# Curvature flow: adding K beside H a period later, one clip for both, another order on ScalarE

## What is computed

```python
def step(u, _):
    ux, uy, uxx, uxy, uyy = _derivs(u)            # Sobel stencils, each clipped to [-10, 10]
    g2 = ux * ux + uy * uy
    denK = jnp.maximum(1.0 + g2, EPS)
    K = jnp.clip((uxx * uyy - uxy * uxy) / (denK * denK + EPS), -5.0, 5.0)
    denH = jnp.sqrt(1.0 + g2 + EPS)
    H = ((1.0 + uy * uy) * uxx - 2.0 * ux * uy * uxy + (1.0 + ux * ux) * uyy) / (2.0 * denH ** 3 + EPS)
    H = jnp.clip(H, -5.0, 5.0)
    diff = jnp.clip(alpha * K + beta * H, -1.0, 1.0)
    u = u + DT * diff
    u = jnp.pad(u[:, :, 1:-1, 1:-1], ((0, 0), (0, 0), (1, 1), (1, 1)), mode='edge')
    return (u, None)
u, _ = jax.lax.scan(step, x, None, length=10)
x1 = 0.7 * u + 0.3 * x
out = conv(relu(conv(x1, w1, b1)), w2, b2) + x1
```

## Time and profile before

| | us |
|---|---|
| median of 3 runs | 38702.86 (38694.59 to 38705.76) |
| profiled execution, its own time | 38698.44 |
| its span | 38696.7 |
| PE busy | 34434.2 (89%) |
| DVE busy | 34434.0 (89%) |
| ACT busy | 33167.9 (86%) |
| POOL busy | 20465.8 (53%) |

### The profile page before, as it was taken

The page is one execution under the profiler, slowest core; times in us unless marked ns, Lnnn a source line. Parts: engine busy times, 40 slices in busy tenths (PEclk is TensorE's granted clock), DMA queues, the critical chain, the costliest instruction groups (busy, mean ns, idle before and its releaser), DMA issues. The chain is left out here.

```text
span 38696.7 us, 453600 instructions
## 1 busy us (share of the span) xinstructions
PE 34434.2 (89%) x126400; PEld 23294.9 (60%) x126400; DVE 34434.0 (89%) x33108; ACT 33167.9 (86%) x33722; POOL 20465.8 (53%) x7685
## 2 busy tenths in 40 slices
PE   5888888888888888888888888888888888889999
PEld 3666666666666666666666666666666666666666
DVE  8999999999999999999999999999999999993111
ACT  5999999999999999999999999999999999994333
POOL 3555555555555556555555555555555555550000
PEclk9999999999999999999999999999999999999999
DMA  5333333333333333333333333333333333333333
GB/s 189 83 83 82 82 75 78 83 83 82 82 83 83 82 79 74 81 83 83 83 82 83 83 83 76 77 81 83 83 83 82 83 83 80 73 82 83 87 87 85
DMA packets 2687511, 3261.71 MB, mean 84 GB/s; under 512 B 2266180, under 2 KB 2266308, under 8 KB 2364740
## 3 DMA queue, kind: packets, MB, share of 16 engines
q1 hardware_dynamic: 2686276, 3247.70, 33.5%
HBM read 582.33 MB, written 268.44 MB: 22 GB/s over the span
## 5 line engine op out<-in xcount | busy, mean ns | idle before, releaser
L646 PE MATMUL tame_slot<-tame_split,tame_M 128*128 128x512 f32 x51200 | 15156.1, 418 | 4131.5 <-DVE tame_ux L517 3386.6
L646 PEld LDWEIGHTS tame_slot<-tame_split,tame_M 128*128 128x128 f32 x51200 | 9160.8, 190 | 10140.8 <-issue 2690.5
L646 PE MATMUL tame_slot<-tame_halo,tame_M 128*128 128x512 f32 x51200 | 14319.2, 402 | 0.0
L356 POOL TENSOR_TENSOR tame_split<-tame_U,tame_split 128x1024 fp32r<-128x1024 f32 x2560 | 6232.0, 2434 | 12755.0 <-ACT tame_split L391 12755.0
L646 PEld LDWEIGHTS tame_slot<-tame_halo,tame_M 128*128 128x128 f32 x51200 | 9757.9, 191 | 2513.8
L368 POOL TENSOR_TENSOR tame_ux<-tame_ux,tame_cross 128x1024 f32<-128x1024 f32 x2560 | 8071.5, 3153 | 433.4 <-POOL tame_ux L362 433.4
L362 POOL TENSOR_TENSOR tame_ux<-tame_ux,tame_uy 128x1024 f32<-128x1024 f32 x2560 | 6161.8, 2407 | 972.6 <-DVE tame_uy L517 972.6
L431 ACT ACTIVATE tame_slope<-tame_slope 128x2048 f32<-128x2048 f32 x2560 | 4895.4, 1912 | 0.0
L656 PE MATMUL tame_slot<-tame_uxy,tame_unit 128*128 128x512 f32 x10240 | 4810.6, 592 | 5.4 <-DVE tame_slot L540 5.4
L426 ACT ACTIVATE tame_slope<-tame_slope 128x1024 f32<-128x1024 f32 x2560 | 2716.8, 1061 | 2141.4 <-issue 2139.4
L559 DVE TENSOR_TENSOR tame_uyy<-tame_slot,tame_slope 128x1024 f32<-128x1024 f32 x2560 | 3132.2, 1223 | 945.6 <-PE tame_slot L656 938.1
(11 more groups left out here) (74 smaller groups left out, 38207.5 us busy)
## 6 DMA issues: line engine op xcount, KB each, us to landing
tame_halo<-tame_split SPq DMA_DIRECT2D x2560, 520.0 KB
tame_halo<-tame_split SPq DMA_DIRECT2D x2560, 260.0 KB
tame_halo<-tame_split SPq DMA_DIRECT2D x5120, 65.0 KB
tame_U<-in_x SPq DMA_DIRECT2D x256, 512.0 KB, 3.9
tame_stage<-in_x SPq DMA_DIRECT2D x128, 1024.0 KB, 4.9
mixed<-tame_stage SPq DMA_DIRECT2D x128, 1024.0 KB, 6.4
out<-res SPq DMA_DIRECT2D x672, 192.0 KB
xin<-mixed SPq DMA_DIRECT2D x344, 256.0 KB, 4.6
```

Of the source, the lines that this page charges most:

```text
L356: nc.gpsimd.tensor_tensor(split_rows(c, 1), half_rows(c), split_rows(c, 0).bitcast(F32), ALU.subtract).then_inc(lo_ready, 2)
L646: last = nc.tensor.matmul(ps[name][:, b * BANK:(b + 1) * BANK], M[0:lanes, matrix, :], rows(c, part)[:, b * y:(b + 1) * y, :], start=(n < ...
```

## The change

- K and H are no longer written over `uyy` and `ux2`, but over the two halves of `slope`, where their inverses lie. One `tensor_scalar` over both halves (`clip_both`) clips them, in place of two.
- add_k moves from the end of the period of chunk k-1 to directly ahead of add_h, one period later. add_h waits for it.
- `uyy` has one buffer instead of two; copy_uyy waits for determinant of the chunk before.
- Waits follow the new owners: square_ux for curvature_h, square_slope for add_k, sum_squares for add_h, each two chunks back.
- ScalarE's order is power, log_power, copy_ux, square_ux, inverse_k, inverse_h, scale, high part, square_uy, copy_uyy, square_slope, square_uxy, logs.

```diff
-        ux2, uy2, cross, uyy = pair("ux2"), pair("uy2"), pair("cross"), pair("uyy")
+        ux2, uy2, cross = pair("ux2"), pair("uy2"), pair("cross")
+        uyy = sb("uyy", [P, HALF])
...
             def square_ux(t, c, fresh):
                 if not fresh:
-                    act.wait_ge(updated, done(t, c - 2))
+                    act.wait_ge(h_ready, done(t, c - 2))
...
-            def copy_uyy(t, c, fresh):
+            def copy_uyy(t, c, first):
                 act.wait_ge(ready["uyy"], done(t, c))
-                if not fresh:
-                    act.wait_ge(k_added, done(t, c - 2))
-                nc.scalar.activation(uyy[c % 2][:, :], ps["uyy"][:, :], ACT.Copy).then_inc(uyy_copied, 2)
+                if not first:
+                    act.wait_ge(prod_k, done(t, c - 1))
+                nc.scalar.activation(uyy[:, :], ps["uyy"][:, :], ACT.Copy).then_inc(uyy_copied, 2)
...
             def square_slope(t, c, fresh):
                 act.wait_ge(slope_ready, done(t, c))
                 if not fresh:
-                    act.wait_ge(k_ready, done(t, c - 2))
+                    act.wait_ge(k_added, done(t, c - 2))
...
                 if exists(kind, k):
                     copy_ux(t, k, fresh)
+                    square_ux(t, k, fresh)
+                if exists(kind, k - 1):
+                    inverse_k(t, k - 1)
+                    inverse_h(t, k - 1, kind == "first" and k == 1)
                 if exists(kind, k - 3) and ends(kind, k - 3):
                     scale(r, k - 3)
-                if exists(kind, k - 1):
-                    inverse_k(t, k - 1)
-                if exists(kind, k):
-                    square_ux(t, k, fresh)
-                    square_uy(t, k, fresh)
-                if exists(kind, k - 1):
-                    inverse_h(t, k - 1, kind == "first" and k == 1)
-                if exists(kind, k):
-                    square_slope(t, k, fresh)
-                    copy_uyy(t, k, fresh)
                 if exists(kind, k - 4) and goes_on(kind, k - 4):
                     next_high(t, k - 4, kind, r)
                 if exists(kind, k):
+                    square_uy(t, k, fresh)
+                    copy_uyy(t, k, first)
+                    square_slope(t, k, fresh)
                     square_uxy(t, k, first)
                     logs(t, k)
...
                 if not fresh:
-                    dve.wait_ge(inv_h_ready, done(t, c - 2))
+                    dve.wait_ge(updated, done(t, c - 2))
                 stt(slope[c % 2][:, 0, :], ux2[c % 2][:, :], 1.0, uy2[c % 2][:, :], ALU.add,
                     ALU.add).then_inc(slope_ready, 2)
...
+                K = slope[c % 2][:, 1, :]
+                nc.vector.tensor_tensor(K, ps["uxx"][:, :], K, ALU.mult).then_inc(k_ready, 2)
...
+                nc.vector.tensor_tensor(slope[c % 2][:, 0, :], ux2[c % 2][:, :], inverse[:, :], ALU.mult).then_inc(
+                    h_ready, 2)
+
+            def clip_both(t, c):
+                both = slope[c % 2][:, :, :]
+                dve.wait_ge(k_ready, done(t, c))
                 dve.wait_ge(h_ready, done(t, c))
-                nc.vector.tensor_scalar(Hh, Hh, CURVATURE_CLIP, -CURVATURE_CLIP, ALU.min, ALU.max).then_inc(h_clipped, 2)
+                nc.vector.tensor_scalar(both, both, CURVATURE_CLIP, -CURVATURE_CLIP, ALU.min, ALU.max).then_inc(
+                    both_clipped, 2)
 
             def add_k(t, c):
-                K = uyy[c % 2][:, :]
-                dve.wait_ge(k_clipped, done(t, c))
+                K = slope[c % 2][:, 1, :]
+                dve.wait_ge(both_clipped, done(t, c))
...
             def add_h(t, c):
-                K, Hh = uyy[c % 2][:, :], ux2[c % 2][:, :]
-                dve.wait_ge(h_clipped, done(t, c))
+                K, Hh = slope[c % 2][:, 1, :], slope[c % 2][:, 0, :]
                 dve.wait_ge(k_added, done(t, c))
...
                 if exists(kind, k - 2):
+                    add_k(t, k - 2)
                     add_h(t, k - 2)
...
                     curvature_h(t, k - 1)
-                    clip_k(t, k - 1)
-                    clip_h(t, k - 1)
-                    add_k(t, k - 1)
+                    clip_both(t, k - 1)
```

More of the change, by code:

```diff
@@ L196, in curvature_flow @@
         k_ready = sem("k_ready")
-        k_clipped = sem("k_clipped")
+        both_clipped = sem("both_clipped")
         h_ready = sem("h_ready")
-        h_clipped = sem("h_clipped")
         k_added = sem("k_added")
@@ L539, in determinant @@
             def determinant(t, c):
-                nc.vector.tensor_tensor(ps["uxx"][:, :], uyy[c % 2][:, :], ps["uxx"][:, :], ALU.mult).then_inc(prod_k, 2)
+                nc.vector.tensor_tensor(ps["uxx"][:, :], uyy[:, :], ps["uxx"][:, :], ALU.mult).then_inc(prod_k, 2)
             def term_uyy(t, c):
@@ L558, in curvature_k @@
                 dve.wait_ge(inv_k_ready, done(t, c))
-                nc.vector.tensor_tensor(uyy[c % 2][:, :], ps["uxx"][:, :], slope[c % 2][:, 1, :],
-                                        ALU.mult).then_inc(k_ready, 2)
-            def clip_k(t, c):
-                K = uyy[c % 2][:, :]
-                dve.wait_ge(k_ready, done(t, c))
-                nc.vector.tensor_scalar(K, K, CURVATURE_CLIP, -CURVATURE_CLIP, ALU.min, ALU.max).then_inc(k_clipped, 2)
+                K = slope[c % 2][:, 1, :]
+                nc.vector.tensor_tensor(K, ps["uxx"][:, :], K, ALU.mult).then_inc(k_ready, 2)
             def curvature_h(t, c):
@@ L569, in curvature_h @@
                 dve.wait_ge(inv_h_ready, done(t, c))
-                nc.vector.tensor_tensor(ux2[c % 2][:, :], ux2[c % 2][:, :], inverse[:, :], ALU.mult).then_inc(h_ready, 2)
-            def clip_h(t, c):
-                Hh = ux2[c % 2][:, :]
+                nc.vector.tensor_tensor(slope[c % 2][:, 0, :], ux2[c % 2][:, :], inverse[:, :], ALU.mult).then_inc(
[3 more added lines that the diff above has]
+                dve.wait_ge(k_ready, done(t, c))
                 dve.wait_ge(h_ready, done(t, c))
-                nc.vector.tensor_scalar(Hh, Hh, CURVATURE_CLIP, -CURVATURE_CLIP, ALU.min, ALU.max).then_inc(h_clipped, 2)
+                nc.vector.tensor_scalar(both, both, CURVATURE_CLIP, -CURVATURE_CLIP, ALU.min, ALU.max).then_inc(
+                    both_clipped, 2)
             def add_k(t, c):
-                K = uyy[c % 2][:, :]
-                dve.wait_ge(k_clipped, done(t, c))
+                K = slope[c % 2][:, 1, :]
+                dve.wait_ge(both_clipped, done(t, c))
                 if tame:
```

## The result

The changed kernel takes 45,097.02 us (median, 45,093.32 to 45,103.08), the kernel before 38,698.72 beside it: ratio 1.1654, 95% interval [1.1633, 1.1674]. The forecast was 44,950, the range 43,100 to 46,200. The profiled execution has a span of 45,101.3 us, 6,405 more than that of before.

The account below looks back on a forecast made before the run. VectorE was taken to set the 13.32 us period. Ordinary periods (15.26 + 0.50) added 5,622 us and blended ones 627: 38,698 + 6,249 = 44,947, rounded 44,950, range 43,100 to 46,200.

Parts of the forecast that it names:

- Part 3: add_h on VectorE: L368, issued earlier, takes over and holds it until about 8.08, 2.08 us of waiting.
- Part 1: Merged clip on VectorE: 1.13 us for two starts' 1.20, saving 0.07; its wait for curvature_h adds 0.11.
- Part 2: add_k on VectorE, moved ahead of add_h: it now gives the 0.16 us to L362, ending at 5.97.
- part 4: VectorE after add_h: curvature_k's wait disappears (-0.50 us), sum_squares waits for square_uy (+0.21); ordinary period 15.26 against 13.32.
- Part 5: ScalarE's new order: high part and inverse_h come before they are wanted; cost nothing, covered by about 3 us idle.
- part 7: TensorE pauses about 2.1 us before uxy; half the ordinary periods get a 3.4 us half-speed stretch: +0.5 us per period.
- Part 6: Blended periods: the low part on GpSimd holds the blend 2.4 us more, giving 17.45 us against 15.00.
- Rival A: Handover from add_h to L368 as forecast, but TensorE's clock stays up: 43,800 us, chance 0.22.
- Rival B: Ports stay with VectorE between add_k and add_h, so L368 does not overtake add_h: 38,280 us, chance 0.11.
- C: Same time within 0.2%: add_h not overtaken, but late square_uy or late clip eats the 0.14 gain: 38,700 us, chance 0.04.

Follow-up runs that it names:

- the merge alone: The changed kernel with add_k back at the end of its own chunk's period and ScalarE's old order: 39,753.74 us, ratio 1.0274 to the kernel before.
- the fourth experiment: The changed kernel with the first four matmuls of the uyy product made twice, inside TensorE's pause: 43,977.43 us, ratio 1.1366 to the kernel before.

## Why the prediction was right

By its own steps:

- **Part 3, the handover**, was right in mechanism and size. add_h was to take 3.3 to 3.4 us and took 3.21, 2.0 us of waiting. That L368 takes over before add_h can be issued is shown from three sides: the waiting disappears when L368 is made to wait; it shrinks by 0.94 us when add_h is issued 0.94 later; and it stays, whatever ScalarE's order. From the merge alone to the same kernel with add_k ahead of add_h, the time rises by 5,009 us.
- **Part 1, the clip**: the duration was right (1.23 us against 1.2), the wait mis-sized. I took 0.03 us behind the forerunner's end, from two tiny instructions of the set-up; at full size it is 0.11 to 0.14. That is the 0.10 by which the short period is longer than forecast (15.36 against 15.26), some 230 us. The Trainium skill, "VectorE: DVE Perf Modes", section "The DRAIN you can't avoid", says that the semaphore costs nothing extra; the traces differ, the merge alone shows 0.2 us per such wait. The clip's saving of 0.07 is smaller than the price of its wait, by three to one.
- **Part 2 and part 4** came out as written: add_k 1.42 us, sum_squares 0.18 idle for square_uy, curvature_k's wait gone.
- **Part 5** put the new ScalarE order at nothing, and in the changed kernel it costs 334 us (44,763 to 45,097). The clock's 0.50 of part 7 hangs on this order: with the old one TensorE has two pauses in place of the long one, 1.03 us for square_ux and 1.38 for square_uy, and its clock stays at 1.00 in ordinary periods, against 0.93; with the clock kept up, at 43,977, the new order is even ahead. In the kernel before the same order costs 22%. Whether the 3 us of ScalarE idle time that I named as its cover make the difference is not shown: that kernel has other waits too (square_ux waits for add_h there).
- **Part 7, the clock**, was right in its mechanism; two errors in size cancelled. I took 0.50 slow stretches per period at 1.0 us each; there are 0.65 at 0.76 (16.12 - 15.36). Both give 0.50, and over the whole trace the ordinary periods are 15.86 us in the mean, 0.50 above the short one. That they meet so closely is luck.
- **Part 6**: blended periods were put at 17.45. The whole is 6,405 us; with 0.10 + 0.50 in the ordinary ones, 2304 x 2.54 = 5,852, some 550 are left for the 256 blended, 17.2. The size was right, the mechanism in part: the blend was to be held by the low part (L356), but it was held in 122 of the 256 only. In most of the others L356 comes after the blend and holds sum_squares instead:
```profile
14464.85 1.22 DVE L514 SCALAR_TENSOR_TENSOR tame_stage<-tame_U,tame_stage 128x1024 f32<-128x1024 f32 x1
14465.25 2.89 POOL L356 TENSOR_TENSOR tame_split<-tame_U,tame_split 128x1024 fp32r<-128x1024 f32 x1 [2.53 <-ACT tame_split L391]
14467.12 2.10 DVE L514 SCALAR_TENSOR_TENSOR tame_slope<-tame_ux,tame_uy 128x1024 f32<-128x1024 f32 x1
```

Rival A, the clock stays up, is what the fourth experiment made, 43,977 against the 43,800 it was put at. Rival B, add_h is not overtaken, did not happen: no add_h that waits for add_k comes ahead of an L368 that is already held, in any of the 2,559 periods. C falls with it.

The trace of the kernel before had a row against B that I overlooked. At the end of the curvature flow there is no multiply_first, so the blend stands directly behind add_h, with L368 held since 34990.23:
```profile
34989.74 1.41 DVE L517 SCALAR_TENSOR_TENSOR tame_U<-tame_ux,tame_par,tame_U 128x1024 f32<-128x1024 f32 x1
34990.23 3.11 POOL L368 TENSOR_TENSOR tame_ux<-tame_ux,tame_cross 128x1024 f32<-128x1024 f32 x1 [0.17 <-POOL tame_ux L362]
34991.07 3.36 DVE L517 SCALAR_TENSOR_TENSOR tame_stage<-tame_U,tame_stage 128x1024 f32<-128x1024 f32 x1
```
The blend does not wait for add_h: it starts 0.08 us before add_h's recorded end, and still it takes 3.36 us, and L368 its usual 3.11. So here a GpSimd operation that was already held got the turn although the next VectorE operation did not wait for the one ahead of it. This suggests that the wait of add_h for add_k is not needed for the loss, and that its place behind add_k, with L368 issued meanwhile, is enough. It is one case, and no run has the two adds without the wait.

## What to carry to other kernels

Where VectorE and GpSimd both work on SBUF, a VectorE operation with two SBUF inputs (add_h, 3.21 us for 1.28) or at double rate (the clip, 1.88 for 1.23) and a GpSimd operation took turns in every run here, so look at who is issued first. Of two such VectorE operations in a row the second lost its turn to a GpSimd operation that was issued during the first, and was held until that ended (in 2,559 periods with a wait between the two, and once without). Put such an operation where GpSimd is idle, or make GpSimd wait for it (3,863 us here). A long mean on an operation of known length is a sign of this, since being held counts as busy, and before reordering a third engine one asks what that does to the turns of the other two: the harmless-looking order of ScalarE cost 22% in the kernel before.

## What the runs showed of the hardware

- A VectorE instruction that waits for the one directly ahead starts 0.11 to 0.14 us after its recorded end, against 0.08 before it without a wait: 0.2 us per dependent pair of 1024 to 2048 elements.
- A GpSimd operation that is held while a two-input operation of VectorE runs goes next: ahead of an add_h that waits (3.21 us for 1.28, 2,559 times) and, once, ahead of a blend that doesn't (3.36 us).
- The double-rate clip, with one SBUF input, is held by a GpSimd operation too: 1.88 us in place of 1.23.
- Pauses of TensorE of 2.25 us are followed by a granted clock of 0.51 for 3.4 us in about two periods of three (0.65 stretches a period in the window of 400 us); with pauses of 1.31 us the ordinary periods stay at 15.36 us. Filling the pause with four matmuls a period, whose result is thrown away, was worth 1,120 us.
